# Expert blocks of 256 rows with the rows stationary, and expert weights gathered by index where the expert changes

## The chip, the cores and the metric

The kernel runs on one core of a Trainium2 chip. The metric is the time of one execution on the device in microseconds (us), as a median over runs. The engines are TensorE (PE), VectorE (DVE), ScalarE (ACT), GpSimd (POOL) and SyncE (SP), each with its own instruction queue; they meet only through semaphores. "PEld" is TensorE loading the stationary operand.

## What is computed

One decoder layer in float32 over x of 4 x 1024 rows of 512 values:

```python
x = x + attention(layernorm(x))            # causal, 16 heads of 64, rotary embedding
x = x + memory_read(layernorm(x), ctx)     # 16 heads of 32; a 32 x 32 memory per head, scanned over 64 context rows
x = x + experts(layernorm(x))
```

The change touches the last line. Every row picks its best two of 8 experts, and an expert is a small gated network:

```python
topk_weights, topk_indices = jax.lax.top_k(x_flat @ router_w + router_b, k=2)
topk_weights = softmax(topk_weights)
# rows sorted by expert
ff_gate = ragged_dot(sorted_tokens, we_gate, group_sizes)     # 512 x 512 per expert
ff_up   = ragged_dot(sorted_tokens, we_up, group_sizes)       # 512 x 512 per expert
ff_out  = ragged_dot(silu(ff_gate) * ff_up, we_down, group_sizes)   # 512 x 512 per expert
output  = zeros.at[sorted_token_idx].add(ff_out * sorted_weights[:, None])
```

So 8192 (row, expert) pairs go through three products of 512 x 512.

## The kernel before

Four phases follow each other with a barrier between them: context_phase, attention_phase, memory_phase and expert_phase. The first two are not touched.

memory_phase ends with the routing. POOL scatters each normalised row twice into a scratch tensor `hs` in HBM, once into the region of each of its two experts (an indirect DMA, L1306). A row there is 516 floats: 512 values, its token number, its top expert, and the gap between its two router values. DVE then makes a table: `nb` is the number of blocks that each expert needs (L1614 to L1617, one comparison per multiple of BLK), and for each block number the table gives the expert and the address of the block's first row (L1622 to L1640). SP waits for the table and writes BLK empty rows behind each expert's last row and into one spare region (9 DMAs, L1245 to L1252), waits for all of them, and the phase ends.

expert_phase walks over NBLK blocks of BLK = 512 rows: 8192/512 + 7 = 23 blocks, a constant that holds whatever the routing is; unused blocks at the end read the spare region and add into spare rows of the output. Everything in a block is float32 done as three passes: each operand is split into a high part (a copy to the float32r type, on ACT) and a low part (the difference, on DVE), and each product is high x high + high x low + low x high (`parts`, L1724 to L1727).

For block j:

- SP loads the rows (`load_rows`, 1 MB) and then three weight matrices of the block's expert (`load_weight`, 1 MB each), one block ahead, each when its buffer is free. It loads them in each block, also when the expert is the same as before.
- PE turns the rows (`turn`, 16 transposes per block), so that `hT` holds the features on the partitions. ACT and DVE split the result.
- PE makes gate and up with the weights stationary and the 512 rows moving: for each of 4 slices of features, 12 matmuls for gate (`G`) and 12 for up (`U`). The result has features on the partitions, as the down product wants it.
- ACT takes silu of gate, DVE multiplies it with up (`a32`), ACT and DVE split that (`aT`). Then `down`: for each of 4 groups of 128 rows 12 matmuls with the rows stationary.
- ACT scales the result by the row's weight (`row_out`, L1782) and POOL adds it to the output in HBM by an indirect DMA with an add (L1706), 128 rows at a time, four per block. After the fourth POOL waits until all have landed (L1709) and raises `added`.
- DVE waits for `added` of the block before (L1845) and only then writes `dest`, the list of output rows, of which there is one buffer.
- ACT splits each weight matrix with one copy of 128x2048 (L1716), DVE with one subtraction of 128x2048 (L1719), three times each per block.

Each engine runs its queue in the order in which the code of its block issues it; no planner reorders. An instruction that waits holds up all that stand behind it on its engine.

## Time and profile before

| | |
|---|---|
| time before, median of 3 runs | 3278.8 us (3277.82 to 3280.2) |
| the profiled execution's own time | 3270.6 us |
| its span, first to last instruction | 3268.8 us |
| busy over the span: DVE, ACT, POOL | 1916.9, 1565.6, 1271.7 us |
| expert phase | about 2423.4 to 3268.8 us |
| mean DMA rate over the span | 117 GB/s |

The span runs from 0 to 3268.8 us; all positions below are microseconds from its start. The profiled execution is one run of the program, 8.2 us shorter than the median. "Busy" is the time in which an engine works on instructions of its own; TensorE's matmuls overlap each other, so that the duration of one (about 0.40 us) is longer than the distance from one to the next. The time before an instruction in square brackets is how long its engine stood idle, with what ended the wait. The granted clock is 1.00 at TensorE's higher level of 2.4 GHz and 0.50 at the lower, 1.2 GHz.

### The profile page before, as it was taken

The numbers are of one execution on the slowest core, as the hardware profiler recorded it, in microseconds if no ns is written. First come the engines' busy times: TensorE is split into PE (matmuls) and PEld (weight loads), VectorE is DVE, ScalarE is ACT, GpSimd is POOL, SyncE is SP. The second block draws the span as 40 slices with busy tenths as digits, with TensorE's granted clock in tenths as the row PEclk, the third lists the DMA queues.
The fourth block names the chain that finished last, engine by engine and source line by source line (L and its number), as shares of the span: only waits on it lengthen the run. The fifth ranks groups of instructions, "written<-read, shape, count | busy, mean of one in ns | idle before, by whom it ended". The sixth has DMA issues, their size and how long they took to land. (4 is left out here: it accounts for less than half of the span.)

```text
span 3268.8 us, 49064 instructions
## 1 busy us (share of the span) xinstructions
PE 2847.5 (87%) x16141; PEld 2364.7 (72%) x16141; DVE 1916.9 (59%) x3699; ACT 1565.6 (48%) x3183; POOL 1271.7 (39%) x1305
## 2 busy tenths in 40 slices
PE   4399998999989999899994888888829999999998
PEld 2288887888778887778873666676628888888886
DVE  5356666666656666566665577777734444444443
ACT  2256665566655666566664232233214444444443
POOL 0256545465454564555643243443301121121121
PEclk8599999999999999999997899999859999999999
DMA  6644334343343433434335344544264555455554
GB/s 183 155 104 97 91 92 103 86 108 87 85 105 84 108 89 84 107 87 103 92 73 130 83 127 115 126 118 118 88 230 129 142 163 145 141 154 154 141 143 127
DMA packets 223734, 383.90 MB, mean 117 GB/s; under 512 B 62592, under 2 KB 129152, under 8 KB 214080
## 3 DMA queue, kind: packets, MB, share of 16 engines
q1 hardware_dynamic: 191520, 290.00, 33.9%
q0 software_dynamic: 32032, 91.63, 11.3%
q8 instruction: 94, 1.54, 0.2%
q14 instruction: 88, 0.72, 0.1%
HBM read 195.17 MB, written 85.70 MB: 86 GB/s over the span
## 5 line engine op out<-in xcount | busy, mean ns | idle before, releaser
L929 ACT ACTIVATE a_pt<-a_PT 128x512 fp32r<-128x512 f32 (+3 forms) x768 | 350.8, 490 | 547.2 <-PE a_PT L819 546.6
L989 DVE TENSOR_REDUCE a_nmax<-a_S 128x1 f32<-128x1024 f32 (+7 forms) x512 | 385.4, 753 | 263.4 <-PE a_S L808 263.3
L998 DVE TENSOR_TENSOR a_pt<-a_PT,a_pt 128x512 fp32r<-128x512 f32 (+3 forms) x768 | 401.5, 550 | 233.1 <-ACT a_pt L929 232.1
L1706 POOL DMA_INDIRECT out<-e_y,e_dest x92 | 162.3, 1765 | 711.1 <-ACT e_y L1784 697.1
L836 PE MATMUL a_O<-a_pt,a_v 128*128 128x256 f32 (+1 forms) x2560 | 353.9, 285 | 52.9 <-DVE a_ot L1013 52.9
L918 ACT ACTIVATE a_pb<-a_S,a_nmax 128x1024 f32<-128x1024 f32 (+7 forms) x512 | 380.7, 744 | 13.8 <-DVE a_nmax L989 13.6
L836 PEld LDWEIGHTS a_O<-a_pt,a_v 128*128 128x128 f32 x2560 | 321.8, 191 | 72.6 <-DVE a_ot L1013 68.1
L819 PE MATMUL a_PT<-a_ident,a_pb 128*128 128x128 f32 x2304 | 342.8, 276 | 32.1 <-DVE a_pt L998 29.0
L819 PEld LDWEIGHTS a_PT<-a_ident,a_pb 128*128 128x128 f32 x2304 | 271.5, 142 | 77.2 <-issue 35.2
L759 PE MATMUL a_Z<-a_xT,a_wq 128*128 128x512 f32 x512 | 242.6, 474 | 67.5 <-POOL a_wq L682 34.0
L806 PE MATMUL a_S<-a_kh,a_qs 128*128 128x512 f32 (+3 forms) x768 | 276.0, 359 | 0.5 <-DMA a_kl<-a_rot 0.5
L707 POOL TENSOR_TENSOR a_rot<-a_tmp,a_rot 128x512 fp32r<-128x512 f32 x128 | 162.6, 1290 | 257.8 <-ACT a_rot L901 257.2
L807 PE MATMUL a_S<-a_kl,a_qs 128*128 128x512 f32 (+3 forms) x768 | 257.9, 348 | 0.0
L699 POOL TENSOR_TENSOR a_tmp<-a_tmp 128x512 f32<-128x512 f32 x64 | 82.7, 1292 | 352.7 <-DVE a_tmp L977 352.7
L1796 ACT ACTIVATE e_aT<-e_a 128x512 fp32r<-128x512 f32 x92 | 58.2, 632 | 312.9 <-DVE e_a L1839 312.9
L761 PE MATMUL a_Z<-a_xT,a_wq 128*128 128x512 f32 x512 | 204.1, 399 | 0.0
L760 PE MATMUL a_Z<-a_xT,a_wq 128*128 128x512 f32 x512 | 203.7, 398 | 0.0
L1719 DVE TENSOR_TENSOR e_w<-e_raw,e_w 128x2048 fp32r<-128x2048 f32 x71 | 162.7, 2292 | 69.3 <-ACT e_w L1716 69.3
L759 PE MATMUL a_Z<-a_wv,a_xT 128*128 128x256 f32 x512 | 164.0, 320 | 2.0 <-DVE a_v L981 2.0
L806 PEld LDWEIGHTS a_S<-a_kh,a_qs 128*128 128x128 f32 x768 | 146.8, 191 | 19.7 <-DMA a_kl<-a_rot 0.9
L807 PEld LDWEIGHTS a_S<-a_kl,a_qs 128*128 128x128 f32 x768 | 146.9, 191 | 18.7
L759 PEld LDWEIGHTS a_Z<-a_xT,a_wq 128*128 128x128 f32 x512 | 101.3, 198 | 80.8 <-issue 48.2
(253 smaller groups left out, 7160.9 us busy)
## 6 DMA issues: line engine op xcount, KB each, us to landing
e_raw<-in_we SPq DMA_DIRECT2D x72, 1024.0 KB, 8.4
a_qs<-a_rot SPq DMA_DIRECT2D x256, 128.0 KB, 2.3
a_kh<-a_rot SPq DMA_DIRECT2D x256, 128.0 KB, 2.3
a_kl<-a_rot SPq DMA_DIRECT2D x256, 128.0 KB, 2.3
e_rows<-scr_hs SPq DMA_DIRECT2D x24, 1032.0 KB, 6.0
a_raw<-in_wqk POOLq DMA_DIRECT2D x32, 512.0 KB, 3.9
scr_attT<-a_ot SPq DMA_DIRECT2D x256, 64.0 KB, 2.1
m_att<-scr_attT SPq DMA_DIRECT2D x32, 512.0 KB, 4.1
```

What stands on the lines that cost most here:

```text
L759: pe.matmul(out, lhs(0), rhs(0), start=start, stop=False)
L760: pe.matmul(out, lhs(0), rhs(1), start=False, stop=False)
L761: return pe.matmul(out, lhs(1), rhs(0), start=False, stop=stop)
L806: pe.matmul(out, q, kh[:, sl, c0:c1], start=True, stop=False)
L807: pe.matmul(out, q, kl[:, sl, c0:c1], start=False, stop=c1 != cols)
L819: mm = pe.transpose(PT[(k + s) % 2][:, (kt % 4) * P:(kt % 4 + 1) * P], pb[u % 2][:, kt * P:(kt + 1) * P], ident[:, :])
L836: mm = pe.matmul(O[:, c0:2 * P], v2[:, n % 2, kt, h, :, :].rearrange("p a d -> p (a d)"), pt[j % 2][:, part, kt, c0:2 * P], start=kt == 0 ...
L918: act.activation(pb[u % 2][:, 0:cols], S[u % 2][:, 0:cols], ACT.Exp, bias=nmax[:, u % GU:u % GU + 1], scale=1.0, accum_out=rsum[:, b % 2, ...
L929: act.activation(pt[u % 2][:, 0, 4 * s:4 * s + m, (qt % 2) * P:(qt % 2 + 1) * P], PT[(k + s) % 2][:, 0:m * P].rearrange("p (k q) -> p k q" ...
L989: dve.tensor_reduce(nmax[:, u % GU:u % GU + 1], S[u % 2][:, 0:cols], AXX, ALU.max, negate=True).then_inc(s_nb, 1)
L998: dve.tensor_tensor(pt[u % 2][:, 1, 4 * s:4 * s + m, q], PT[(k + s) % 2][:, 0:m * P].rearrange("p (k q) -> p k q", k=m), pt[u % 2][:, 0, 4 ...
L1719: eng.tensor_tensor(w[:, k, 1, :], raw[:, k, :], w[:, k, 0, :].bitcast(F32), ALU.subtract).then_inc(s["wlo"], 1)
```

## The change

- BLK is 256. There are 8192/256 + 7 = 39 blocks, each with two groups (t = 0, 1) of 128 rows.
- Gate and up have the rows stationary and the weights moving, as down had before: per group 12 matmuls of 128x512 for gate and 12 for up (`product`). The result now has the rows on the partitions, so PE must turn `a32` before down (`turn_act`, 4 transposes per group).
- The weight loads leave SP. POOL issues them as indirect DMAs (`fetch`), with one index per partition from the table `source`; where block j has the same expert as block j-1 the index lies out of bounds (SKIP is added) and the DMA moves nothing. The index of the fetch is copied by POOL from the table (`point`).
- The queue orders on PE, ACT and DVE are new; the low half of a weight is made in two subtractions of 128x1024. In POOL's loop the two adds of a block are separated by a wait for the first (`st0`), the waits for the fetches, `point` and two fetches.
- The number of blocks per expert is counted with two DVE instructions instead of eight; tables are 42 wide instead of 32. The empty rows that SP writes are 256 per region.

```diff
 
 NE = 8
-BLK = 512
+BLK = 256
 REG = TOK + BLK
 NBLK = (2 * TOK) // BLK + NE - 1
+NTAB = NBLK + 3
 EPS = 1e-5
...
-            ch.step(dve.tensor_scalar(nb[:, :], cnt[:, :], 0.0, None, ALU.is_gt))
-            for m in range(1, TOK // BLK):
-                ch.step(dve.scalar_tensor_tensor(out=nb[:, :], in0=cnt[:, :], scalar=float(m * BLK), in1=nb[:, :],
-                                                 op0=ALU.is_gt, op1=ALU.add))
+            ch.step(dve.tensor_tensor(over[:, :, :], cnt[:, :].unsqueeze(2).broadcast_to([P, NE, TOK // BLK]),
+                                      thr[:, :].unsqueeze(1).broadcast_to([P, NE, TOK // BLK]), ALU.is_gt))
+            ch.step(dve.tensor_reduce(nb[:, :], over[:, :, :], AXX, ALU.add))
...
-        hT = rm.sb("hT", [P, 2, ET, BLK], F32R)
...
-        aT = rm.sb("aT", [P, 2, ET, BLK], F32R)
+        hT = rm.sb("hT", [P, RT, 2, D], F32R)
+        sil = rm.sb("sil", [P, RT, D])
+        a32 = rm.sb("a32", [P, RT, D])
+        aT = rm.sb("aT", [P, RT, 2, D], F32R)
...
+        CR = 2
+        HALF = WM // 2
+        SKIP = 1 << 16
...
-            e0 = entry(0, 0, NE - 1)
-            for k in range(3):
-                load_weight(k, e0)
             with sp.Fori(0, NBLK) as j:
-                e = entry(0, j + 1, NE - 1)
-                wait_alone(sp, s["tlo"], 4 * j + 4 + 2, s["any"])
+                wait_alone(sp, s["Th"], 2 * j + 2, s["any"])
+                wait_alone(sp, s["nxt"], j + 1, s["any"])
                 load_rows(j + 1)
-                for k in range(2):
-                    wait_alone(sp, s["wlo"], 3 * j + k + 1, s["any"])
-                    load_weight(k, e)
-                wait_alone(sp, s["wlo"], 3 * j + 3, s["any"])
-                load_weight(2, e)
-            for k in ("rows", "rawg", "rawu", "rawd"):
-                sp.wait_ge(s[k], 16 * (NBLK + 1))
+            sp.wait_ge(s["rows"], 16 * (NBLK + 1))
 
...
+            gp.iota(part[:, :], pattern=[[0, 1]], base=0, channel_multiplier=1).then_inc(s["part"], 1)
+            gp.wait_ge(s["part"], 1)
+            gp.tensor_copy(partf[:, :], part[:, :]).then_inc(s["part"], 1)
+            gp.wait_ge(s["src"], 7)
+
+            we = io["we"].rearrange("e k p n -> (e k p) n")
+
+            def point(j):
+                gp.tensor_copy(ix[:, :].unsqueeze(2), source[:, :, bass.ds(j, 1)]).then_inc(s["ix"], 1)
+
+            def fetch(k):
+                gp.indirect_dma_start(raw[:, k, :], None, we, bass.IndirectOffsetOnAxis(ap=ix[:, k:k + 1], axis=0),
+                                      bounds_check=NE * 3 * P - 1, oob_is_err=False).then_inc(s[f"raw{k}"], 16)
+
+            def add_rows(t):
+                gp.indirect_dma_start(io["out"][:, :],
+                                      bass.IndirectOffsetOnAxis(ap=dest[:, t:t + 1], axis=0),
+                                      y[:, t, :], None, compute_op=ALU.add).then_inc(s[f"st{t}"], 16)
+
+            point(0)
+            gp.wait_ge(s["ix"], 1)
+            for k in range(3):
+                fetch(k)
+            for k in range(3):
+                gp.wait_ge(s[f"raw{k}"], 16)
+            point(1)
+            gp.wait_ge(s["ix"], 2)
+            for k in range(2):
+                wait_alone(gp, s[f"wlo{k}"], 2, s["any"])
+                fetch(k)
             with gp.Fori(0, NBLK) as j:
-                for t in range(RT):
-                    wait_alone(gp, s["y"], 4 * j + t + 1 + 2, s["any"])
-                    gp.indirect_dma_start(io["out"][:, :],
-                                          bass.IndirectOffsetOnAxis(ap=dest[:, t:t + 1], axis=0),
-                                          y[:, t, :], None, compute_op=ALU.add).then_inc(s["st"], 16)
-                gp.wait_ge(s["st"], 16 * RT * j + 16 * RT)
+                wait_alone(gp, s["wlo2"], 2 * j + 2, s["any"])
+                fetch(2)
+                wait_alone(gp, s["y"], 2 * j + 1 + CR, s["any"])
+                add_rows(0)
+                wait_alone(gp, s["st0"], 16 * j + 16, s["any"])
+                for k in range(3):
+                    wait_alone(gp, s[f"raw{k}"], 16 * j + 32, s["any"])
+                point(j + 2)
+                wait_alone(gp, s["ix"], j + 3, s["any"])
+                for k in range(2):
+                    wait_alone(gp, s[f"wlo{k}"], 2 * j + 4, s["any"])
+                    fetch(k)
+                wait_alone(gp, s["y"], 2 * j + 2 + CR, s["any"])
+                add_rows(1)
+                gp.wait_ge(s["st1"], 16 * j + 16)
                 gp.sem_inc(s["added"], 1)
...
+            def turn_act(j, t):
+                pe.wait_ge(s["mul"], 2 * j + t + 1 + CR)
+                pe.wait_ge(s["alo"], 2 * j + t + CR)
+                for f in range(ET):
+                    mm = pe.transpose(pT[0][:, f * P:(f + 1) * P], a32[:, t, f * P:(f + 1) * P], ident[:, :])
+                mm.then_inc(s["Ta"], 1)
+
+            def product(j, k, out, t, sem):
+
+                if t == 0:
+                    pe.wait_ge(s[f"wlo{k}"], 2 * j + 2)
+                if k == 0:
+                    pe.wait_ge(s["tlo"], 2 * j + t + 1 + CR)
+                    pe.wait_ge(s["mul"], 2 * j + t - 1 + CR)
+                for e in range(ET):
+                    mm = parts(out[t][:, :], lambda a: hT[:, t, a, e * P:(e + 1) * P],
+                               lambda a: w[:, k, a, e * D:(e + 1) * D], e)
+                mm.then_inc(s[sem], 1)
...
+                product(j, 0, pG, 0, "G")
+                product(j, 1, pU, 0, "U")
+                product(j, 0, pG, 1, "G")
+                turn_act(j, 0)
+                product(j, 1, pU, 1, "U")
+                turn_rows(j + 1, 0)
+                down(j, 0, 0, 2)
+                turn_act(j, 1)
+                down(j, 0, 2, ET).then_inc(s["Y"], 1)
+                turn_rows(j + 1, 1)
+                down(j, 1, 0, ET).then_inc(s["Y"], 1)
...
+            def act_high(j, t):
+                act.wait_ge(s["Ta"], 2 * j + t + 1)
+                act.wait_ge(s["Y"], 2 * j + t - 1 + CR)
+                act.activation(aT[:, t, 0, :], pT[0][:, :], ACT.Copy).then_inc(s["ahi"], 1)
+
+            def weight_high(j, k, done):
+                act.wait_ge(s[f"raw{k}"], 16 * (j + 1))
+                act.wait_ge(s[done], 2 * j + CR)
+                act.activation(w[:, k, 0, :], raw[:, k, :], ACT.Copy).then_inc(s[f"whi{k}"], 1)
...
+                act.wait_ge(s["added"], j + 1)
+                act.activation(y[:, t, :], pY[t][:, :], ACT.Copy, scale=wt[:, t:t + 1]).then_inc(s["y"], 1)
...
+                weight_high(j, 2, "Y")
+                silu(j, 0)
+                silu(j, 1)
+                act_high(j, 0)
+                weight_high(j + 1, 0, "G")
                 turn_high(j + 1, 0)
+                act.wait_ge(s["arg"], j + 1)
+                act.activation(gate[:, :], arg[:, :], ACT.Tanh).then_inc(s["gate"], 1)
+                act_high(j, 1)
+                weight_high(j + 1, 1, "U")
+                act.wait_ge(s["wt"], j + 1)
+                row_out(j, 0)
                 turn_high(j + 1, 1)
-                split(act, j + 1, 0, 0)
-                act.wait_ge(s["wt"], j + 1)
-                for t in range(2):
-                    row_out(j, t)
-                    turn_high(j + 1, t + 2)
-                split(act, j + 1, 1, 0)
-                for t in range(2, RT):
-                    row_out(j, t)
+                row_out(j, 1)
...
+            def act_low(j, t):
+                dve.wait_ge(s["ahi"], 2 * j + t + 1)
+                dve.tensor_tensor(aT[:, t, 1, :], pT[0][:, :], aT[:, t, 0, :].bitcast(F32),
+                                  ALU.subtract).then_inc(s["alo"], 1)
+
+            def weight_low(j, k, h):
+                dve.wait_ge(s[f"whi{k}"], j + 1)
+                c = slice(h * HALF, (h + 1) * HALF)
+                dve.tensor_tensor(w[:, k, 1, c], raw[:, k, c], w[:, k, 0, c].bitcast(F32),
+                                  ALU.subtract).then_inc(s[f"wlo{k}"], 1)
...
+            ch = Chain(dve, s["src"])
+            ch.do(dve.memset(same[:, 0:1], 0.0))
+            ch.step(dve.tensor_tensor(same[:, 1:NTAB], route["expert"][:, 1:NTAB], route["expert"][:, 0:NTAB - 1],
+                                      ALU.is_equal))
+            ch.step(dve.tensor_scalar(first[:, :], route["expert"][:, :], float(3 * P), None, ALU.mult))
+            ch.step(dve.scalar_tensor_tensor(out=first[:, :], in0=same[:, :], scalar=float(SKIP), in1=first[:, :],
+                                             op0=ALU.mult, op1=ALU.add))
+            dve.wait_ge(s["part"], 2)
+            for k in range(3):
+                dve.tensor_scalar(source[:, k, :], first[:, :], partf[:, 0:1], float(k * P), ALU.add,
+                                  ALU.add).then_inc(s["src"], 1)
...
+                for h in range(2):
+                    weight_low(j, 2, h)
+                mult(j, 0)
+                dve.wait_ge(s["added"], j + 1)
+                dve.wait_ge(s["nxt"], j + 1)
+                dve.tensor_copy(dest[:, :], nxt[:, :, 0]).then_inc(s["side"], 1)
+                dve.tensor_tensor(side[:, :], nxt[:, :, 1],
+                                  route["expert"][:, bass.ds(j, 1)].broadcast_to([P, RT]),
+                                  ALU.is_equal).then_inc(s["side"], 1)
+                dve.wait_ge(s["side"], 2 * j + 2)
+                dve.scalar_tensor_tensor(out=arg[:, :], in0=side[:, :], scalar=-0.5, in1=nxt[:, :, 2],
+                                         op0=ALU.add, op1=ALU.mult).then_inc(s["arg"], 1)
+                act_low(j, 0)
+                mult(j, 1)
+                dve.wait_ge(s["arg"], j + 1)
+                keep_side(j + 1)
+                weight_low(j + 1, 0, 0)
+                turn_low(j + 1, 0)
+                act_low(j, 1)
                 dve.wait_ge(s["gate"], j + 1)
                 dve.tensor_scalar(wt[:, :], gate[:, :], 0.5, 0.5, ALU.mult, ALU.add).then_inc(s["wt"], 1)
...
+                weight_low(j + 1, 0, 1)
+                for h in range(2):
+                    weight_low(j + 1, 1, h)
+                turn_low(j + 1, 1)
```

## Rows read from the trace of the kernel before

**Rows 1.** The page: busy time of the engines over the span.
```profile
PE 2847.5 (87%) x16141; PEld 2364.7 (72%) x16141; DVE 1916.9 (59%) x3699; ACT 1565.6 (48%) x3183; POOL 1271.7 (39%) x1305
```
**Rows 2.** Stretches: bounds, length, busy per engine (instructions), clock, DMA share, GB/s.
```profile
2060.00:2100.00 40.00, 34.27 (x175) 27.21 (x174) 31.71 (x80) 11.78 (x22) 18.85 (x13) 1.00 0.54 132
...
2424.00:2439.00 15.00, 3.88 (x16) 3.00 (x16) 4.94 (x6) 6.20 (x7) 0.00 (x0) 0.50 0.79 296
...
2600.00:2635.30 35.30, 35.30 (x161) 28.59 (x160) 15.48 (x20) 16.25 (x22) 7.05 (x4) 1.00 0.53 149
```
**Rows 3.** The chain that ended last: start, length, what.
```profile
2439.35 0.80 PE e_G L1725
...
2494.28 0.44 PE e_T L1733 x4
...
2529.59 0.44 PE e_T L1733 x4
...
3250.85 0.45 PE e_T L1733 x4
```
**Rows 4.** Timeline of PE: first matmuls of two series of 12.
```profile
2709.19 0.39 PE L1725 MATMUL e_U<-e_hT,e_w 128*128 128x512 f32 x1
...
2711.98 0.40 PE L1725 MATMUL e_Y<-e_w,e_aT 128*128 128x512 f32 x1
```
**Rows 5.** Groups by line from 2200 us on: count, busy, mean ns, idle before.
```profile
L1719 DVE TENSOR_TENSOR e_w<-e_raw,e_w 128x2048 fp32r<-128x2048 f32 x71 | 162.7, 2292 | 69.3 <-ACT e_w L1716 69.3
...
L1716 ACT ACTIVATE e_w<-e_raw 128x2048 fp32r<-128x2048 f32 x71 | 135.4, 1908 | 0.0
...
L1842 DVE TENSOR_TENSOR e_aT<-e_a,e_aT 128x512 fp32r<-128x512 f32 x92 | 63.7, 692 | 64.3 <-ACT e_aT L1796 64.3
...
L1796 ACT ACTIVATE e_aT<-e_a 128x512 fp32r<-128x512 f32 x92 | 58.2, 632 | 312.9 <-DVE e_a L1839 312.9
```
**Rows 6.** Timeline of POOL: the first and third of the four adds of one block.
```profile
2648.02 1.56 POOL L1706 DMA_INDIRECT out<-e_y,e_dest  x1 [24.47 <-ACT e_y L1784]
...
2654.61 2.39 POOL L1706 DMA_INDIRECT out<-e_y,e_dest  x1 [3.16 <-ACT e_y L1784]
```
**Rows 7.** Timeline of ACT: the copy that releases the first of these adds.
```profile
2646.52 0.69 ACT L1784 ACTIVATE e_y<-e_Y,e_wt 128x512 f32<-128x512 f32 x1 [0.83 <-PE e_Y L1727]
```
**Rows 8.** DMA issues: us from issue to landing (adds at 3248.50, 3255.10, 2586.69).
```profile
out<-e_y,e_dest POOLq DMA_INDIRECT x1, 4.6
...
out<-e_y,e_dest POOLq DMA_INDIRECT x1, 5.3
...
out<-e_y,e_dest POOLq DMA_INDIRECT x2, 10.4
```
**Rows 9.** Timeline of DVE: after `added` of the block before.
```profile
2668.32 0.17 DVE L1847 CAST e_dest<-e_nxt 128x4 int32<-128x4 f32 x1 [7.01 <-POOLq L1710]
...
2668.78 0.69 DVE L1839 TENSOR_TENSOR e_a<-e_U,e_sil 128x512 f32<-128x512 f32 x1
```
**Rows 10.** Tile scr_hs: duration ns min/median/max of POOL's plain scatter.
```profile
L1306 POOL DMA_INDIRECT scr_hs<-m_hn,m_pi x64: 959/1256/1712, 1886.4 to 2384.9; - x64
```
**Rows 11.** Timeline of SP around the empty rows: start, time to issue.
```profile
2395.12 13.21 SPq L1248 DMA_DIRECT2D scr_hs<-m_zero  x8
...
2423.40 0.35 SPq L1684 DMA_DIRECT2D e_ident<-in_ident  x1
...
2425.71 0.36 SPq L1681 DMA_DIRECT2D e_raw<-in_we  x1
```
**Rows 12.** Timeline of DVE: the count of blocks per expert.
```profile
2382.26 1.37 DVE L1616 SCALAR_TENSOR_TENSOR m_nb<-m_cnt,m_nb 128x8 f32<-128x8 f32 x7
```
**Rows 13.** The last add, and POOL's smallest cast (mean ns 215).
```profile
3257.79 1.55 POOL L1706 DMA_INDIRECT out<-e_y,e_dest  x1 [0.30 <-issue]
...
L1269 POOL CAST m_itf<-m_it 128x32 f32<-128x32 int32 x1 | 0.2, 215 | 0.0
```
**Rows 14.** Waits of PE, 1900 to 2380 us: total, times, longest.
```profile
PE m_T L1340 <- DVE m_nT L1506: 37.1, 22, 4.1
```

More of the change, by code:

```diff
@@ L76, in program @@
         route = {
[L77 to L78 removed]
+            "expert": keep.enter_context(nc.sbuf_tensor("expert", [P, NTAB], F32)),
+            "tab": keep.enter_context(nc.sbuf_tensor("tab", [P, 4, NTAB], I32)),
         }
@@ L1656, in expert_phase @@
         dest = rm.sb("dest", [P, RT], I32)
-        hT = rm.sb("hT", [P, 2, ET, BLK], F32R)
-        sil = rm.sb("sil", [P, 2, BLK])
-        a32 = rm.sb("a32", [P, 2, BLK])
-        aT = rm.sb("aT", [P, 2, ET, BLK], F32R)
+        hT = rm.sb("hT", [P, RT, 2, D], F32R)
+        sil = rm.sb("sil", [P, RT, D])
+        a32 = rm.sb("a32", [P, RT, D])
+        aT = rm.sb("aT", [P, RT, 2, D], F32R)
         y = rm.sb("y", [P, RT, D])
         ident = rm.sb("ident", [P, P])
+        part = rm.sb("part", [P, 1], I32)
+        partf = rm.sb("partf", [P, 1])
+        same = rm.sb("same", [P, NTAB])
+        first = rm.sb("first", [P, NTAB])
+        source = rm.sb("source", [P, 3, NTAB], I32)
+        ix = rm.sb("ix", [P, 3], I32)
         pT, pG, pU, pY = ([rm.ps(f"{n}{i}", [P, 512]) for i in range(2)] for n in "TGUY")
-        names = "any id rows rawg rawu rawd whi wlo T thi tlo G U sil mul ahi alo Y y st added nxt side arg gate wt".split()
+        names = ("any id rows raw0 raw1 raw2 whi0 whi1 whi2 wlo0 wlo1 wlo2 Th thi tlo Ta ahi alo G U sil mul "
+                 "Y y st0 st1 added nxt side arg gate wt part src ix").split()
         s = {k: rm.sem(k) for k in names}
+        CR = 2
+        HALF = WM // 2
+        SKIP = 1 << 16
         block = rm.ctx.enter_context(nc.Block())
@@ L1712, in split @@
-        def split(eng, j, k, part):
-            if part == 0:
-                eng.wait_ge(s[("rawg", "rawu", "rawd")[k]], 16 * (j + 1))
-                eng.activation(w[:, k, 0, :], raw[:, k, :], ACT.Copy).then_inc(s["whi"], 1)
-            else:
-                eng.wait_ge(s["whi"], 3 * j + k + 1)
-                eng.tensor_tensor(w[:, k, 1, :], raw[:, k, :], w[:, k, 0, :].bitcast(F32),
-                                  ALU.subtract).then_inc(s["wlo"], 1)
+            gp.iota(part[:, :], pattern=[[0, 1]], base=0, channel_multiplier=1).then_inc(s["part"], 1)
@@ L1722, in _ @@
+            for k in range(2):
+                gp.wait_ge(s[f"raw{k}"], 16 * (NBLK + 2))
+            gp.wait_ge(s["raw2"], 16 * (NBLK + 1))
         @block.tensor
@@ L1778, in turn_high @@
-            def turn_high(j, e):
-                act.wait_ge(s["T"], 4 * j + e + 1)
-                act.activation(hT[:, 0, e, :], pT[e % 2][:, :], ACT.Copy).then_inc(s["thi"], 1)
-            def row_out(j, t):
-                act.wait_ge(s["Y"], 4 * j + t + 1 + 1)
-                act.activation(y[:, t, :], pY[t % 2][:, :], ACT.Copy, scale=wt[:, t:t + 1]).then_inc(s["y"], 1)
-            for e in range(ET):
-                turn_high(0, e)
-            split(act, 0, 0, 0)
-            split(act, 0, 1, 0)
@@ new lines, in silu @@
+            def silu(j, t):
+                act.wait_ge(s["G"], 2 * j + t + 1 + CR)
+                act.activation(sil[:, t, :], pG[t][:, :], ACT.Silu).then_inc(s["sil"], 1)
+            def row_out(j, t):
+                act.wait_ge(s["Y"], 2 * j + t + 1 + CR)
+                act.wait_ge(s["added"], j + 1)
+                act.activation(y[:, t, :], pY[t][:, :], ACT.Copy, scale=wt[:, t:t + 1]).then_inc(s["y"], 1)
+            for t in range(RT):
+                turn_high(0, t)
+            weight_high(0, 0, "G")
@@ L1828, in keep_side @@
                 dve.tensor_copy(nxt[:, :, :], rows[:, :, D:HW]).then_inc(s["nxt"], 1)
-            keep_side(0)
-            for e in range(ET):
-                turn_low(0, e)
-            split(dve, 0, 0, 1)
-            split(dve, 0, 1, 1)
-            with dve.Fori(0, NBLK) as j:
-                for f in range(ET):
-                    dve.wait_ge(s["U"], 4 * j + f + 1)
-                    dve.wait_ge(s["sil"], 4 * j + f + 1)
-                    dve.tensor_tensor(a32[:, f % 2, :], pU[f % 2][:, :], sil[:, f % 2, :],
-                                      ALU.mult).then_inc(s["mul"], 1)
-                    dve.wait_ge(s["ahi"], 4 * j + f + 1)
-                    dve.tensor_tensor(aT[:, 1, f, :], a32[:, f % 2, :], aT[:, 0, f, :].bitcast(F32),
-                                      ALU.subtract).then_inc(s["alo"], 1)
-                    if f == 0:
-                        dve.wait_ge(s["added"], j + 1)
-                        dve.wait_ge(s["nxt"], j + 1)
-                        dve.tensor_copy(dest[:, :], nxt[:, :, 0]).then_inc(s["side"], 1)
-                        dve.tensor_tensor(side[:, :], nxt[:, :, 1],
-                                          route["expert"][:, bass.ds(j, 1)].broadcast_to([P, RT]),
-                                          ALU.is_equal).then_inc(s["side"], 1)
-                        dve.wait_ge(s["side"], 2 * j + 2)
-                        dve.scalar_tensor_tensor(out=arg[:, :], in0=side[:, :], scalar=-0.5, in1=nxt[:, :, 2],
-                                                 op0=ALU.add, op1=ALU.mult).then_inc(s["arg"], 1)
-                    if f == 1:
-                        split(dve, j, 2, 1)
```

121 lines of the change are left out of this document (45 added, 76 removed).

## The prediction

> **What bounds the kernel now.** I read the page first: TensorE is busy for 87% of the span and everything else for less than 60% [rows 1]. Then the stretches of the expert phase, since only that phase and the end of the one before it are edited. In a stretch of one block TensorE is busy for all of 35.30 us at clock 1.00, while DVE and ACT are busy for less than half and POOL for 7 us [rows 2]. The chain that ended last says the same: from the first gate matmul at 2439.35 on it runs along TensorE, and the same group of transposes returns after 35.31 us [rows 3]. Twelve matmuls of 128x512 take 2711.98 - 2709.19 = 2.79 us, 0.2325 us each [rows 4]. A block has 144 of them, 33.5 us; the other 1.8 us are its four groups of transposes, 0.46 us each. So 23 blocks cost 23 x 35.31 = 812 us, and TensorE is the only bound. Weights, splits and adds are hidden. POOL's adds are hidden too, though not short: each lands 4.6 to 5.3 us after its issue, and 10.4 us where weight loads are in flight [rows 8], and DVE stands 7.01 us before `dest` until the fourth has landed [rows 9]. Nobody on TensorE's side feels that in a block of 35 us.
>
> **TensorE's own work.** A new block has 2 x (12 + 12 + 12) = 72 matmuls, 16.74 us, and four groups of transposes (two for the rows, two for the activations), 1.83 us: 18.57 us. Thirty-nine blocks are 724 us against 812. Which operand is stationary doesn't change the price: both kinds of product were 128x512 before and cost the same [rows 4]. If TensorE stayed the bound, this would be worth 88 us.
>
> **Where I think it goes wrong: a cycle through POOL.** `dest` still has one buffer, so the DVE steps that make it and the row weights wait for both adds of the block before. Behind that wait in DVE's queue stand `act_low(j,0)` and the rest of the block, and TensorE's down product waits for them. Before, the adds followed each other. Now add 1 stands behind the landing of add 0, `point` and two fetches, in each block, also where the fetches move nothing. I follow one round, from `added`:
>
> 1. DVE sees `added` (0.20) and runs its three small instructions, 2668.78 - 2668.32 = 0.46 [rows 9]: 0.66.
> 2. `act_low(j,0)` 0.69 [rows 5] and the hand-over 0.05: 0.74.
> 3. TensorE: 6 matmuls of down, 1.40, then `turn_act(j,1)`, 0.46, and until ACT sees it 0.2: 2.06. (`mult(j,1)`, 0.69 on DVE, lies beside the six.)
> 4. ACT: `act_high(j,1)` 0.63, `weight_high(j+1,1)` 1.91 [rows 5], `row_out(j,0)` 0.69 [rows 7]: 3.23. The other half of down lies beside it.
> 5. The add starts 0.81 us after that copy ends (2646.52 + 0.69 to 2648.02) [rows 6, 7]. It then runs beside DVE's subtractions of the weights, as the third add did, 2.39 instead of 1.56 us [rows 6], so I take the landing of 5.3 [rows 8]: 6.11.
> 6. Three waits for the fetches, `point` (a copy of three values; POOL's small cast takes 0.22 [rows 13]) and its wait: 0.6.
> 7. Two fetches. No gather and no skipped DMA is in this trace. The nearest row is POOL's plain scatter with 128 indices, 0.96 when nothing disturbs it [rows 10]. Start 0.81, 0.96, gap 0.30 [rows 13], 0.96, gap 0.30: 3.33.
> 8. Add 1 with nothing in flight: 4.8, between 4.6 and 5.3 [rows 8].
>
> The sum is 21.5 us. That is more than TensorE's 18.57, so the cycle sets the pace and TensorE stands idle for 2.9 us per block, ahead of its down product.
>
> The bounds of the unknown term (7): a skipped fetch could cost as little as the small cast, 0.22, which takes 2 x 0.74 = 1.5 us off the round; it could cost as much as an add, 1.56, which puts 1.2 us on, or a disturbed add, 2.39, 2.9 us on. I keep 0.96: it is a DMA with as many indices and no addition. The landings, 4.6 twice or 5.4 twice, move the round by -0.9 to +0.8.
>
> Where the expert changes (7 times) 2 MB lie in the queue ahead of add 1. The fourth add took 10.4 - 4.8 = 5.6 us longer beside 3 MB of loads [rows 8]; two thirds of that is 3.7 us, 26 us in all. The third fetch is issued a third of a round ahead of the next add and I give it nothing. The bounds are 0 and 7 x 5.6 = 39 us. That the other fetches move nothing (8 x 3 MB in all instead of 24 x 3) helps no one: the loads were hidden.
>
> The splits: ACT and DVE now split 3 weights per 18 to 21 us, ACT 3 x 1.91 and DVE 3 x 2.29 us [rows 5]; with their 512-wide steps that is some 11 us on each. They fit, except for the 1.91 us that stands in step 4. If TensorE set the pace that too would cost nothing.
>
> **What is saved around it.** The empty rows: 9 DMAs of 1 MB ran from 2395.12 to 2423.40 with nothing beside them [rows 11]. Half of the data, at the same rate, saves half of the 25 us of flow, 12.6 us; bounds 11 and 14. The block counts: seven comparisons took 1.37 us [rows 12] and there was an eighth; two instructions replace them: -1.0. The start: SP issued its first weight 2.3 us after the phase began [rows 11] and the first gate matmul came at 2439.35, after 15.95 us [rows 3]. POOL needs the table `source` first, seven short DVE steps of about 0.22 us and one copy, and issues at about 2.8 us; but the rows are half as many to bring and turn, and the first weight need not wait behind 4 turns: -2, bounds -4 and +2. The extra POOL step at the start of memory_phase is some 0.25 us against a memset of half the size: nothing.
>
> **The sum.** First gate matmul: 2439.35 - 12.6 - 1.0 - 2.0 = 2423.7. The clock is at its lower level there [rows 2]; before, the last group of transposes (3250.85) and the 12 matmuls behind it ended at 3254.1, 2.6 us later than 2439.35 + 812.1 [rows 3], so the slow start costs 2.6. Block 0 has no `added` to wait for and its first `row_out` ends 17.3 us after its start (TensorE's share 15.3, then ACT). 38 rounds of 21.5: 817. Expert changes: 26. From the last `row_out(.,0)` to the landing of the last add, steps 5 to 8: 14.8. From there to the end of the span: before, the last add was issued at 3257.79 and landed about 5.1 later, 5.9 before the end [rows 13]. In all 2423.7 + 2.6 + 17.3 + 817 + 26 + 14.8 + 5.9 = 3307.3. Against 3268.8 this is 38.5 us more. The profiled execution took 3270.6 us and would take 3309; the median of the runs shown is 8.2 us above it, so I forecast 3278.8 + 38.5 = 3317 us.
>
> A sentence of the Trainium skill speaks against this cycle: "DMA: Bandwidth & Descriptors", section "Anatomy of one DMA — SWDGE (gpsimd) path", gives one DMA issued by GpSimd as about 2.0 us plus its bytes over 436 GB/s. For 256 KB that is an estimate of 2.6 us, against the 4.6 from issue to landing that this trace has for an add in a quiet stretch, so here they differ. By the page two landings would take 4.9 us less together and TensorE would stay the bound; I go by the row, which holds the add itself.
>
> **Rivals.**
>
> - TensorE stays the bound. For this the round must fall under 18.57, 2.9 us less than I have: cheap skips (-1.5), quick landings (-0.9) and a hand-over or two that I counted and that overlaps. Then 39 x 18.57 = 724, and the end is 2423.7 + 2.6 + 724 + 6.5 (last copy and add) + 5.9 = 3162.9: 106 us less, 3173 us. For it speaks that no row shows a skipped fetch; against it, that the two landings, the add's own and TensorE's part are measured. The page above would make this case.
> - The cycle binds, but a skipped fetch costs 0.22. 38 x 1.5 = 57 us less than the forecast: 3260 us. The round at which the change breaks even is 38.5/38 = 1.0 us shorter than mine, 20.5.
> - A fetch costs as an add does, 1.56: 46 us more, 3363 us.
> - The change doesn't do what it says: the out-of-bounds fetches move their data all the same. Then add 1 lands 3.7 us later in 31 more blocks: 3432 us. It would show as 3 MB of DMA in each block.
> - The clock. The idle stretch of 2.9 us lies just ahead of step 3. If the clock fell to its lower level in each, step 3 would take 1.9 us more: 3388 us. Against it: in memory_phase TensorE had gaps of up to 4.1 us [rows 14], and a stretch with 34 of 40 us busy still shows 1.00 [rows 2].
>
> **Chances.** The cycle near 21.5 (3285 to 3350) 0.50; a dearer fetch 0.13; fetches that move data or the lower clock 0.05; cheap skips 0.16; TensorE the bound 0.16. About 0.2%, 6.6 us, is what can be told from no change here. The cheap-skip case lies mostly below 3272, with a little of it in the band: faster 0.29, same 0.06, slower 0.65. The range reaches from 3235, which takes in the cheap-skip case with short landings and leaves out TensorE as the bound, to 3375. The likeliest case's own range is 3285 to 3350.
>
> **What would show it.** Right: DVE waits for `added` in each block, right after the first multiplication; TensorE's longest wait is for DVE's low half of `aT`, about 2.9 us in each block; the distance from block to block is 21 to 22 us, longer at 7 of them; POOL's two fetches lie between the two adds; the empty rows take about 15 us; the clock stays at 1.00. Wrong: blocks 18.6 us apart with TensorE busy throughout (then the round is shorter than my rows make it), a fetch that takes well under or over 0.96 us where nothing moves, or TensorE waiting for `wlo` (then the weights come too late, which I gave nothing).

## The result, and the profile after

The changed kernel takes 3406.16 us (median of 4 runs, 3401.72 to 3412.1) against 3279.5 us for the kernel before in the same job: a ratio of 1.0388, 95% interval 1.0367 to 1.0408. It is slower, as forecast, but by 127 us instead of 38. The profiled execution is the longest of the four, 3412.1 us, with a span of 3410.6 us.

The page of the changed kernel: busy time, the slices of TensorE and its clock, and the chain that ended last by engine.

```profile
PE 2828.8 (83%) x15885; PEld 2341.1 (69%) x15885; DVE 1985.9 (58%) x3903; ACT 1700.1 (50%) x3244; POOL 1422.8 (42%) x1457
...
PE   4399989999899998999957888887488887878786
...
PEclk7599999999999999999988988998799998999998
...
DMA 13%; PE 6%; issue 5%; POOL 3%; DVE 1%; ACT 1%; POOLq 0%; ACTq 0%; SPq 0%
```

The same row of TensorE in the page of the kernel before:

```profile
PE   4399998999989999899994888888829999999998
```

The reader is to see that the last quarter of the span, the expert phase, has fallen from nearly full slices to 7 and 8, that the clock is uneven there, and that the chain now runs through DMA and POOL, where it ran along TensorE before [rows 3]. The waits of the expert phase (total, times, longest) say who waits:

```profile
DVE e_dest L1915 <- POOLq L1745: 316.9, 38, 11.6
...
POOL out L1714 <- ACT e_y L1836: 237.3, 39, 10.9
...
PE e_Y L1753 <- DVE e_aT L1871: 164.8, 38, 7.6
POOL e_ix L1707 <- DMA out<-e_y,e_dest: 152.0, 39, 4.5
```

DVE waits in each of 38 blocks for `added`, and TensorE as often for the low half of `aT`, 4.3 us on average. One round, from `dest` to `dest`, on the timelines of DVE, ACT and POOL:

```profile
2645.81 0.17 DVE L1915 CAST e_dest<-e_nxt 128x2 int32<-128x2 f32 x1 [7.87 <-POOLq L1745]
...
2646.19 0.68 DVE L1871 TENSOR_TENSOR e_aT<-e_T,e_aT 128x512 fp32r<-128x512 f32 x1
...
2651.67 3.50 DVE L1877 TENSOR_TENSOR e_w<-e_raw,e_w 128x1024 fp32r<-128x1024 f32 x3
...
2658.95 2.36 DVE L1877 TENSOR_TENSOR e_w<-e_raw,e_w 128x1024 fp32r<-128x1024 f32 x2 [3.18 <-ACT e_w L1827]
```
```profile
2650.37 0.60 ACT L1822 ACTIVATE e_aT<-e_T 128x512 fp32r<-128x512 f32 x1 [3.86 <-PE e_T L1768]
2650.86 1.91 ACT L1827 ACTIVATE e_w<-e_raw 128x2048 fp32r<-128x2048 f32 x1
2652.67 0.68 ACT L1836 ACTIVATE e_y<-e_Y,e_wt 128x512 f32<-128x512 f32 x1
```
```profile
2654.19 2.43 POOL L1714 DMA_INDIRECT out<-e_y,e_dest  x1 [6.14 <-ACT e_y L1836]
2660.39 0.97 POOL L1707 COPY e_ix<-e_source 128x3 int32 x1 [3.77 <-DMA out<-e_y,e_dest]
2662.40 1.06 POOL L1710 DMA_INDIRECT e_raw<-in_we,e_ix  x1 [1.04 <-issue]
2663.76 0.99 POOL L1710 DMA_INDIRECT e_raw<-in_we,e_ix  x1 [0.31 <-issue]
2665.06 1.61 POOL L1714 DMA_INDIRECT out<-e_y,e_dest  x1 [0.30 <-issue]
```

The next `dest` comes at 2670.05, 24.24 us after the first. Read POOL's rows in order: add 0, its landing, the index copy, two fetches that move nothing (the expert stays) but still take 1.06 and 0.99 us, add 1. Add 0 and the copy each lie beside DVE's subtractions of weights (2651.67 and 2658.95) and are long, 2.43 and 0.97 us. The long add was in my sum (2.39), the long copy was not. Nor was a second thing: TensorE restarts slowly. This is TensorE in the following round, after its idle stretch, and some 9 us later:

```profile
2671.17 0.80 PE L1753 MATMUL e_Y<-e_w,e_aT 128*128 128x512 f32 x1 [4.14 <-DVE e_aT L1871]
...
2673.90 1.05 PE L1768 MATMUL e_T<-e_ident,e_a 128*128 128x128 f32 x4
...
2680.46 0.39 PE L1753 MATMUL e_G<-e_w,e_hT 128*128 128x512 f32 x1
2680.69 0.40 PE L1754 MATMUL e_G<-e_w,e_hT 128*128 128x512 f32 x1
```

From the first matmul to the transposes, six matmuls, it takes 2.73 us, against 6 x 0.23 = 1.4 at the end. It is not so in each round. In the round after this one the gap is 2.70 us and the same six take 1.50:

```profile
2695.40 0.50 PE L1753 MATMUL e_Y<-e_w,e_aT 128*128 128x512 f32 x1 [2.70 <-DVE e_aT L1871]
...
2696.90 0.60 PE L1768 MATMUL e_T<-e_ident,e_a 128*128 128x128 f32 x4
```

Of the 37 rounds with a gap, ten have one of 2.70 to 3.05 us and six matmuls in 1.49 to 1.51 us; the eleventh in that range takes 1.66, and 25 with a gap of 3.63 us or more take 2.19 to 2.73. The stretches of the three rounds from 2645.80 on (the columns of [rows 2]) show the clock:

```profile
2645.80:2670.05 24.25, 20.10 (x88) 16.03 (x88) 11.16 (x17) 13.04 (x14) 8.09 (x6) 0.93 0.26 43
2670.05:2694.50 24.45, 21.52 (x88) 17.17 (x88) 11.39 (x19) 13.03 (x14) 7.57 (x6) 0.86 0.26 43
2694.28:2717.00 22.72, 18.81 (x88) 15.10 (x88) 11.16 (x18) 13.04 (x14) 8.01 (x6) 1.00 0.27 46
```

### The profile page after: what moved, and what is told of

Its sections match the earlier page's. It is cut to its first block and busy times, and to the rows that moved or that the text cites. A ratio compares the mean times of both kernels' runs of the same rounds, so it can differ in the third digit from the quotient of the medians.

```text
span 3410.6 us, 49814 instructions
## 1 busy us (share of the span) xinstructions
PE 2828.8 (83%) x15885; PEld 2341.1 (69%) x15885; DVE 1985.9 (58%) x3903; ACT 1700.1 (50%) x3244; POOL 1422.8 (42%) x1457
## 5 line engine op out<-in xcount | busy, mean ns | idle before, releaser
L1877 DVE TENSOR_TENSOR e_w<-e_raw,e_w 128x1024 fp32r<-128x1024 f32 x238 | 280.5, 1220 | 138.3 <-ACT e_w L1827 138.3
L760 PE MATMUL a_Z<-a_xT,a_wq 128*128 128x512 f32 x512 | 243.1, 475 | 69.5 <-POOL a_wq L683 36.1
L1753 PE MATMUL e_Y<-e_w,e_aT 128*128 128x512 f32 x312 | 154.9, 496 | 164.8 <-DVE e_aT L1871 164.8
L1714 POOL DMA_INDIRECT out<-e_y,e_dest x78 | 153.8, 1972 | 249.2 <-ACT e_y L1836 237.3
L1827 ACT ACTIVATE e_w<-e_raw 128x2048 fp32r<-128x2048 f32 x119 | 227.7, 1913 | 29.2 <-DMA e_raw<-in_we,e_ix 28.8
L1710 POOL DMA_INDIRECT e_raw<-in_we,e_ix x122 | 125.7, 1030 | 256.0 <-issue 251.5
L1753 PEld LDWEIGHTS e_Y<-e_w,e_aT 128*128 128x128 f32 x312 | 69.0, 221 | 184.5 <-DVE e_aT L1871 173.8
```

The costliest lines, as they stand in the source:

```text
L760: pe.matmul(out, lhs(0), rhs(0), start=start, stop=False)
L1753: pe.matmul(out, lhs(0), rhs(0), start=k == 0, stop=False)
L1827: act.activation(w[:, k, 0, :], raw[:, k, :], ACT.Copy).then_inc(s[f"whi{k}"], 1)
L1877: dve.tensor_tensor(w[:, k, 1, c], raw[:, k, c], w[:, k, 0, c].bitcast(F32), ALU.subtract).then_inc(s[f"wlo{k}"], 1)
```

## The experiments

All times but the last experiment's are medians of 4 runs, the ratios against the kernel before on the same chip. "Round" is the median distance between the `side` steps of successive blocks (24.33 us in the changed kernel, 35.28 before).

**The cycle is cut in two ways.** First, a table for `dest`, so that DVE does not wait for `added`:

```diff
-                dve.wait_ge(s["added"], j + 1)
-                dve.tensor_copy(dest[:, :], nxt[:, :, 0]).then_inc(s["side"], 1)
+                dve.tensor_copy(dests[:, bass.ds(j, 1), :], nxt[:, :, 0].unsqueeze(1)).then_inc(s["side"], 1)
...
+                wait_alone(gp, s["side"], 2 * j + 2, s["any"])
+                gp.tensor_copy(dest[:, :].unsqueeze(1), dests[:, bass.ds(j, 1), :]).then_inc(s["dc"], 1)
+                wait_alone(gp, s["dc"], j + 1, s["any"])
                 wait_alone(gp, s["y"], 2 * j + 1 + CR, s["any"])
```

> The list of output rows gets a table with one entry per block, so DVE no longer waits for both adds of the block before; GpSimd copies its entry ahead of the first add. The y buffers are still guarded by added. Theory A (the cycle from added through DVE, TensorE's down, ACT, add, fetches, add sets the pace of 24.4 us): the cycle is cut; what is left is GpSimd's own loop, 6.24 (add 0) + 1.95 + 2.66 (point, fetches) + 4.75 (add 1) + 3.4 (third fetch, copy, starts) = about 19.0 us per block, so the time falls by 5.3 x 38 = 200 us to about 3200 us. Rival B (the block is long because DVE and ACT have too much work in a bad order: two table loads, nine splits): nothing changes, 3400 us. Rival C (the lower clock after each gap makes the block long by itself): the gap goes with the wait, so it gives the same sign as A but at most 1.4 us per block if the gap stayed.

Measured: 3242.77 us, ratio 0.9883 (0.9866 to 0.9899); the round is 18.95 us. The wait was the pace. The mean of the rounds is 20.2, so 43 us of the forecast gain did not come. ACT stands 54.2 us in all ahead of its copies of fetched weights in that trace, and another 63.3 us ahead of the table loads that come before such a copy; the seven rounds with an expert change in them are 24.0 to 28.0 us long.

Second, the order of the adds; `dest` stays as it is:

```diff
                 add_rows(0)
+                wait_alone(gp, s["y"], 2 * j + 2 + CR, s["any"])
+                add_rows(1)
                 wait_alone(gp, s["st0"], 16 * j + 16, s["any"])
+                gp.wait_ge(s["st1"], 16 * j + 16)
+                gp.sem_inc(s["added"], 1)
...
-                wait_alone(gp, s["y"], 2 * j + 2 + CR, s["any"])
-                add_rows(1)
-                gp.wait_ge(s["st1"], 16 * j + 16)
-                gp.sem_inc(s["added"], 1)
```

> The two adds of a block are issued one behind the other, as before the change, and point and the first two fetches come after both have landed. dest keeps its one buffer. Theory A: from row_out to added it is 0.84 + 2.43 + 0.3 + 5.3 = 8.9 instead of 16.6 us, the round falls to about 16 us, below TensorE's 18.6; the pace is 18.6 to 19 us and the time falls by about 5.9 x 38 = 225 us to about 3180 us, faster than the kernel before. Rival B (ACT's and DVE's order): 3400 us, no change. Rival D (the fetches are what costs, wherever they stand): they still take their 2.7 us on GpSimd, so the time falls by less than half of that.

Measured: 3210.84 us, ratio 0.9790 (0.9768 to 0.9812). The round is 18.92 us, in most blocks 18.4 to 19.1. Moving two instructions in one queue is worth 195 us. B and D fall: no splitting and no fetch was taken away. Its POOL timeline for one block:

```profile
2527.71 1.89 POOL L1714 DMA_INDIRECT out<-e_y,e_dest  x1 [4.90 <-ACT e_y L1836]
2530.46 1.58 POOL L1714 DMA_INDIRECT out<-e_y,e_dest  x1 [0.86 <-ACT e_y L1836]
2535.82 0.21 POOL L1707 COPY e_ix<-e_source 128x3 int32 x1 [3.77 <-DMA out<-e_y,e_dest]
```

From add 0 to the index copy behind the landing of both it is 8.1 us here (8.5 in the median); in the changed kernel add 1 alone was issued 10.9 us after add 0.

**The clock.** Twelve matmuls whose result is overwritten go where TensorE would wait:

```diff
                 turn_rows(j + 1, 0)
+                pe.wait_ge(s["y"], 2 * j - 1 + CR)
+                for e in range(ET):
+                    parts(pY[0][:, :], lambda a: hT[:, 1, a, e * P:(e + 1) * P],
+                          lambda a: w[:, 1, a, e * D:(e + 1) * D], e)
                 down(j, 0, 0, 2)
```

> Twelve matmuls whose result is thrown away are put where TensorE waits for the low half of aT, so that it does not stand idle for 4 us there. Nothing else changes. Theory A with the clock as one of its terms: TensorE's clock stays at 1.00, the six matmuls of down and the four transposes take 1.48 instead of 2.72 us, the round falls by 1.2 us and the time by 40 to 50 us, to about 3360 us, although TensorE does 2.8 us more work per block. Rival (the clock fell for another reason or does not count): no change, or slower by up to 2.8 x 39 = 109 us if TensorE were the bound.

Measured: 3382.49 us, ratio 1.0305 (1.0281 to 1.0330), 24 us less than the changed kernel, with 12 more matmuls per block. In a stretch of 100 us:

```profile
2662.97 0.50 PE L1753 MATMUL e_Y<-e_w,e_aT 128*128 128x512 f32 x1 [1.36 <-DVE e_aT L1875]
```
```profile
2640.00:2740.00 100.00, 91.49 (x421) 73.11 (x422) 48.12 (x75) 53.75 (x58) 33.19 (x25) 0.98 0.34 74
```

The gap is 1.36 instead of some 4 us, the clock 0.98, the six matmuls take 1.50 instead of 2.72 us, and the round 22.96. So the fall of the clock after the gap costs 1.4 us in the rounds that have it. The gain was half of what I expected because not every round is one of them: the mean round went from 24.65 to 23.95 only. The six matmuls took over 1.6 us in 26 of 38 rounds of the changed kernel; with the filler they still do in 8: in the first, and in the seven behind an expert change, where a gap of 4.3 to 5.2 us is left.

**Fetches that move their data.** Nothing else is changed.

```diff
-        SKIP = 1 << 16
+        SKIP = 0
```

> Nothing is added to the index where the expert stays the same, so every fetch moves its 1 MB. Theory A: the fetches of the changed kernel really move nothing where the expert stays; here add 1 stands behind 2 MB in each block as it does at the 7 changes, where it lands 3.5 us later: 31 x 3.5 = 108 us more, about 3515 us, and more if the third fetch delays add 0. Rival (skipped fetches move data anyway, or cost as much): no change, 3406 us.

Measured: 3529.14 us, ratio 1.0749 (1.0731 to 1.0767). The step from add 1 to `dest` has a median of 8.29 us, against 4.95; in the changed kernel it is that long only where the expert changes. The queue of GpSimd's DMAs moved 215.9 MB in the whole execution, against 113.2 in the changed kernel: 102.7 MB more, which is 98 weights of 1 MB. So the skip does what it says, and in this order of the adds it is worth 123 us; in the kernel before the loads were hidden.

**Fetches ahead of the adds.** In e2 seven blocks are still 21.9 to 23.6 us long: ACT's queue stands at a gate weight that has not landed, here for 5.19 us:

```profile
2502.45 1.91 ACT L1827 ACTIVATE e_w<-e_raw 128x2048 fp32r<-128x2048 f32 x1 [5.19 <-DMA e_raw<-in_we,e_ix]
```

```diff
+                for k in range(3):
+                    wait_alone(gp, s[f"raw{k}"], 16 * j + 32, s["any"])
+                point(j + 2)
+                wait_alone(gp, s["ix"], j + 3, s["any"])
+                wait_alone(gp, s["wlo0"], 2 * j + 4, s["any"])
+                fetch(0)
                 wait_alone(gp, s["y"], 2 * j + 1 + CR, s["any"])
                 add_rows(0)
                 wait_alone(gp, s["y"], 2 * j + 2 + CR, s["any"])
                 add_rows(1)
+                wait_alone(gp, s["wlo1"], 2 * j + 4, s["any"])
+                fetch(1)
```

> As e2 (adds together), but the index copy and the gate fetch for block j+2 go ahead of the two adds and the up fetch right behind them, instead of all behind their landing. Theory A says that e2 is bound by TensorE (blocks of 18.4 to 19.0 us) except for 7 blocks of 22 to 23.6 us in which ACT waits for a gate weight that was fetched too late. Here that weight is issued some 10 us sooner: the seven long blocks shrink to about 19 us, 7 x 3.6 = 25 us less than e2, about 3186 us. Rival (the long blocks come from the adds standing behind 2 MB of fetches): the fetches still share the queue with the adds, so the long blocks stay, 3211 us; and if the 1.3 us ahead of add 0 brings the cycle through added above 18.6 us, slower than e2 in every block.

Measured: 3176.1 us, ratio 0.9676 (0.9658 to 0.9694), the fastest kernel of this study. The round is 18.42 us, its mean 18.56, and the seven long blocks are 20.2 to 22.2 us. That is not the 19 us that I expected, yet the time is 10 us below the 3186 that I expected. The blocks are measured on DVE, and TensorE does not stand still in the long ones: from 2440 to 3160 us it has no idle time at all, where e2 has 22.9 us between 2440 and 3190. A stretch of 100 us:

```profile
2700.00:2800.00 100.00, 100.00 (x475) 81.35 (x474) 60.47 (x92) 68.86 (x76) 43.46 (x33) 1.00 0.43 89
```

TensorE is the bound again, at the 18.57 us per block of my sum. The first rival had 3173 us for that case. That rival's price of a block was right; the changed kernel is just not in its case. That its total is within 3 us is in part luck: the span here, 3175.3 us, is 12.4 above the 3162.9 of that rival, about the 11.8 by which the first gate matmul is later (2435.48 against 2423.7). Which of the moved instructions (the index copy, the gate fetch, the up fetch) brings the gain was not separated.

**Blocks of 256 rows alone.** The kernel before with 39 blocks, the counters adapted to two groups of rows, the last two `turn`s behind `down`, tables 42 wide.

```diff
-BLK = 512
+BLK = 256
...
-                            mm = parts(out[f % 2][:, :],
+                            mm = parts(out[f % 2][:, 0:BLK],
...
-                for t in range(2, RT):
-                    turn(j + 1, t)
-                    pe.wait_ge(s["y"], 4 * j + t - 1 + 2)
-                    down(t, 0, ET).then_inc(s["Y"], 1)
+                turn(j + 1, 2)
+                turn(j + 1, 3)
```

> The kernel before with BLK = 256 alone: weights stationary for gate and up with 256 rows moving, SP loading 3 MB in each block, the two adds together. It tells what the rows-stationary part is worth. By TensorE's rows a matmul of 256 columns can't be issued faster than its weight load of 0.188 us: 96 x 0.19 + 24 x 0.2325 + 8 transposes, about 24.7 us per block, 39 x 24.7 = 963 against 812 us, less 13 us for the shorter empty rows: about 3420 us. Rival (the loads are hidden and 256 columns cost half of 512, 0.116 us): 17.6 us per block on TensorE, and the time is below 3250 us or set by another engine.

Measured: 3488.83 us, ratio 1.0633 (1.0613 to 1.0652), a round of 27.07 us. Two matmuls and a gap of its TensorE:

```profile
2705.08 0.28 PE L1728 MATMUL e_G<-e_hT,e_w 128*128 128x256 f32 x1
2705.20 0.28 PE L1726 MATMUL e_G<-e_hT,e_w 128*128 128x256 f32 x1
...
2709.60 0.79 PE L1726 MATMUL e_Y<-e_w,e_aT 128*128 128x512 f32 x1 [2.11 <-DVE e_aT L1839]
```

My mechanism was wrong. A matmul of 256 columns comes every 0.118 us, half of 0.2325, though its weight load lasts 0.188: the loads overlap. TensorE's share of this block is 96 x 0.118 + 24 x 0.2325 + 0.9 = 17.8 us. The rest is waits of TensorE (for `hT` 69.5 us in 38, for the weights' low halves 67.1, for `aT` 88.0) with a lower clock among them (0.87 and 0.91 in two stretches). DVE stands 144.1 us in 38 for `added` here too, so the wait of the changed kernel stands in this one as well, though its adds are together; whether it sets the pace here was not tried. So what rows-stationary gives by itself is not shown: on the array it saves nothing and adds 0.9 us of transposes; whether it helps the order of the queues, this kernel, whose orders were not rewritten, can't tell.

**DVE's subtractions out of POOL's way.** Each covers one column of 1024; the low halves of the weights are thus not made. (The low half of the down weight is set to 0 once, ahead of the loop.)

```diff
-                c = slice(h * HALF, (h + 1) * HALF)
+                c = slice(h * HALF, (h + 1) * HALF) if isinstance(j, int) else slice(h * HALF, h * HALF + 1)
```

> The changed kernel, but DVE's subtractions for the low halves of the weights in the loop cover one column instead of 1024 each (six of about 0.1 us instead of 1.22 us); the other low columns are left as they were, which changes the values. The waits and the order are kept. Theory A with the stretched GpSimd instructions as one of its terms: add 0 (2.43 us) and point (0.99 us) lie beside these subtractions; without them add 0 takes 1.57 us and point 0.19 us, the round falls by 1.6 us from 24.3 to 22.7 us, and where the shorter gap keeps TensorE's clock up by another 1.2 us: 65 to 100 us less, 3305 to 3340 us. Rival (add 0 and point are long for another reason, the rows' load or the queue): both keep their durations and the time stays within 20 us of 3406, since DVE's work is not on the cycle.

Measured: 3342.22 us, ratio 1.0184 (1.0167 to 1.0201), 64 us less; the round is 22.64 us. POOL's timeline:

```profile
2659.51 1.57 POOL L1714 DMA_INDIRECT out<-e_y,e_dest  x1 [4.84 <-ACT e_y L1836]
2664.93 0.18 POOL L1707 COPY e_ix<-e_source 128x3 int32 x1 [3.85 <-DMA out<-e_y,e_dest]
```

Both are as short as expected, so the subtractions are what stretches them. Not all of the 64 us is theirs, though: the gap falls with the round, to 2.46 us in the median, and TensorE's step between the start of the six matmuls and `act_high` falls from 3.50 to 2.63.

The Trainium skill has this rule ("SBUF — State Buffer", section "Who interferes with whom"): a DVE instruction with two inputs in SBUF contends with a GpSimd instruction that reads SBUF. For the index copy the trace agrees: 0.97 us beside the subtractions in the block shown above, 0.18 without. For the add the same section of the Trainium skill infers otherwise, that such a `tensor_tensor` does not hold up the generation of a DMA's descriptors. Here the add takes 2.43 us beside them and 1.57 without: page and measurement differ, and the measurement decides.

**The kernel before once more**, for its first three phases: one run, 3285.79 us.

> The kernel before once more, for a second trace of its first three phases. In the trace of the changed kernel the empty rows are issued 10.1 us later than in the trace of before, although little was edited ahead of them. If that is a difference between executions, this trace has them anywhere between 2395 and 2407 us; if it comes from the change, they stand at 2395 us again.

SP issues the empty rows at 2409.20 in that trace, at 2405.25 in the trace of the changed kernel:

```profile
2409.20 13.21 SPq L1248 DMA_DIRECT2D scr_hs<-m_zero  x8
```
```profile
2405.25 10.08 SPq L1251 DMA_DIRECT2D scr_hs<-m_zero  x8
```

Against 2395.12 in the first [rows 11] that is 14.1 us between two executions of one kernel, 2 us beyond the bound that I had given. The 10.1 us by which the changed kernel is late there are within that. The other six kernels that share its first three phases (e1 to e5 and e8) have this row at 2398.74 to 2407.39, on both sides of 2405.25.

## Why the prediction was right in kind and wrong in size

The sum ended at 3307.3, the span is 3410.6: 103 us more. (By the medians, 3317 forecast and 3406 measured, it is 89: the profiled execution was 8.2 us below its median before and is 5.9 above it now.) The first gate matmul came at 2435.30 instead of 2423.7, of which 10.1 is the difference between executions just told. The 38 rounds took 936.6 us (2443.3 to 3379.9) instead of 817 + 26: 93.6 more. The rest is 2 us less than forecast. So the loss sits in the round, by its own steps; measured values are taken over the 38 rounds from the timelines:

| step | predicted | median | mean |
|---|---|---|---|
| 1, 2: `added` seen, `act_low` | 1.40 | 1.12 | 1.24 |
| 3: six matmuls, `turn_act`, hand-over | 2.06 | 3.50 | 3.16 |
| 4: `act_high`, `weight_high`, `row_out` | 3.23 | 2.98 | 3.06 |
| 5 to 7: add 0, its landing, `point`, two fetches | 10.04 | 11.71 | 11.63 |
| 8: add 1 to `dest` | 4.8 (5.5 with the expert changes) | 4.95 | 5.56 |
| sum | 21.5 (22.2) | 24.3 | 24.65 |

By the means, steps 5 to 7 make 60 us of the 93.6 and step 3 makes 42; the other steps take 9 off.

- **The cycle: right.** DVE waits in each block, TensorE ahead of its down product, the two fetches lie between the adds. e1 and e2 show that it is the bound: with it cut the round is 18.9 us.
- **Step 3: mis-sized by 1.44 us in the median and 1.1 on average, and it was a rival that I gave 0.05 together with another.** I held the lower clock unlikely because memory_phase had gaps of up to 4.1 us and a stretch at 1.00 [rows 2, 14]. But those 4.1 us were the longest of 22 gaps, and other stretches of that phase have 0.87 to 0.96. The other misjudgment fed it: the gap grows with the round, to 4.0 us in the median and not the 2.9 that I had, since the steps below were longer too. Where it was near 2.9 (2.70 to 3.05, eleven rounds) this step took 2.12 to 2.15 in ten, which is what I had; but that is no rule, since in e8 it took so in 17 of 30 rounds with gaps of 2.0 to 3.2, and 2.61 to 3.33 in the other 13. e3 gives the term by itself.
- **Steps 5 to 7: mis-sized by 1.67 us, the larger miss.** I counted the long third add [rows 6] and took 5.3 for its landing, which is that of one single add [rows 8]; add 0 lands after 5.64 in the median. From there to the start of `point` it is another 0.59, and from there to the first fetch 1.95, together 2.54 where steps 6 and 7 had 1.41. `point` I priced by a quiet copy, 0.22, without asking what would run beside it; it takes 0.90 in the median, and e8 shows that the subtractions of the down weight do that. Why they lie there is argued from the rows only: ACT loads a function table twice per block (1.28 us each, ahead of `weight_high(j,2)` and of silu; it was once before), which my sum leaves out. Without the first of them the subtractions at 2658.95 would end 1.28 us sooner, about 2660.0, ahead of the copy at 2660.39. e8 takes 1.16 us of the mean round off these steps, and the shorter gap another 0.46 off step 3.
- **The fetch without data: right.** 0.96 was taken, 0.99 to 1.06 measured. The rivals with a cheap or a dear skip fall with it, and e4 shows that the skipped ones move nothing.
- **Expert changes: right.** From add 1 to `dest` it is 8.20 to 9.10 us in those seven rounds, 3.3 to 4.1 more than in the others; 3.7 was taken (from 10.4 us [rows 8], which stands for two adds of 10.2 and 10.5). The gap behind such a round is 7.1 to 7.6 us.
- **What is saved around it: right.** The empty rows took 16.15 us to the next phase instead of 28.28 (12.1 saved, 12.6 taken), the start of the phase 13.90 instead of 15.95 us.
- **TensorE's own work: right.** 18.57 us per block is what e5 runs at, 18.56.

What stays open: what rows-stationary is worth by itself (e6), and why 0.59 us pass from the landing of add 0 to the start of `point`, in the changed kernel and in e8 alike, where less than 0.1 us passes from the landing of add 1 to `dest`. Four waits stand in POOL's queue there, but no run took them out. The landing itself is not the difference: in e8, where nothing stretches the issue, it is 5.06 us for add 0 and 4.86 for add 1.

## What to carry to other kernels

When a block is halved, everything that happens once per block with a latency of its own (two landings of 5 us, a few waits in a queue) has half the time to hide in: write down the round that runs through the single-buffered item and compare it with the bound engine's share before halving. In such a round, two transfers that wait for each other cost their landings twice; issue them together and put what doesn't depend on them elsewhere in the queue. That order alone turned 1.039 into 0.979 here, and moving the index copy and the two fetches made it 0.968.

And a gap on TensorE that lies in such a round can lengthen the round once more, through the slower matmuls that follow: 1.4 us in the rounds where it did so here. A longer round makes a longer gap, so the two misses feed each other.

## What the runs showed of the hardware

- An indirect DMA whose 128 indices are all out of bounds keeps POOL for 0.99 to 1.06 us in the changed kernel's loop and has a median of 2.2 us from issue to landing. With its data (e4) the median is 1.03 us on POOL and 7.5 us to landing. Saving the data does not save the instruction. In e5, where the fetches stand elsewhere in the queue, they take up to 2.08 us; one of 2.05 us (2719.98) starts 0.1 us behind a pair of DVE's subtractions (2719.88).
- After a gap of 4.14 us TensorE's next matmuls came every 0.43 us, the lower level, and at full rate again only after 5.9 us of work. After other gaps of 3.6 us and more in the same trace it came back after 2.9 to 6.2 us. After a gap of 2.70 us, and after the 1.36 us of e3, they kept their rate.
- A matmul of 256 columns with a new 128x128 stationary operand each time came every 0.118 us, within 2% of half the time of one of 512 (0.2325), although the load of that operand lasts 0.188.
- Beside DVE's subtractions of 128x1024 with both inputs in SBUF, the indirect add kept POOL for 2.43 us instead of 1.57 and the copy of 128x3 for 0.97 instead of 0.18 (e8).
